# Another order of weighing, adding and score chain, and longer rings, in the edge passes of the first two layers of a graph network

## The reference

```python
# first layer, for each of 2 heads (D = 128), grouped by source node
score = s_src[src] + s_dst[dst]
e = jnp.exp(-jnp.where(score > 0, score, ALPHA * score))
row_sum = segment_sum(e, src);  num = segment_sum(e[:, None] * h[dst], src)
out = elu(num / row_sum[:, None])
...
# second layer, 8 heads of 32, grouped by destination node
alpha = edge_weight[:, None] * (alpha_l[src] + alpha_r[dst])
alpha = jnp.where(alpha > 0, alpha, 0.2 * alpha)
ex = jnp.exp(alpha - segment_max(alpha, dst)[dst])
agg = segment_sum(x[src] * (ex / (segment_sum(ex, dst)[dst] + 1e-16))[:, :, None], dst)
```

## Time and profile before

| | |
|---|---|
| median of 3 runs | 6146.24 us (6140.39 to 6148.77) |
| the profiled execution's own time | 6137.13 us |
| its span | 6135.2 us |
| first layer's edge pass: first gather, last gather, last add | 842.09, 1444.44, 1470.59 us |
| second layer's edge pass: the same | 2214.1, 2820.01, 2864.52 us |
| busy: PE, DVE, ACT, POOL | 3529.9, 3292.3, 1408.6, 3409.4 us |

### The profile page before, as it was taken

How to read it: one execution, slowest core, us unless ns; L and a number is a source line. 1 busy time by engine, 2 the same in 40 slices (tenths; PEclk the granted TensorE clock), 3 DMA queues, 4 the chain that set the end, 5 groups by cost and what they waited for, 6 DMA issues and landing times. The chain is left out here.

```text
span 6135.2 us, 56916 instructions
## 1 busy us (share of the span) xinstructions
PE 3529.9 (58%) x14811; PEld 2769.4 (45%) x14811; DVE 3292.3 (54%) x6546; ACT 1408.6 (23%) x3123; POOL 3409.4 (56%) x3358
## 2 busy tenths in 40 slices
PE   0365237774300067774677775887777667955551
PEld 0265126663100056663455553775555466434441
DVE  7497325555300047767678887347888742122225
ACT  0000112221200022221355553334555332200000
POOL 3778777776788747773066663005666400057771
PEclk9755656775655558876889997998999888977776
DMA  1043134443200034543277775016777610333333
GB/s 42 2 107 75 28 78 130 127 128 51 51 2 2 3 89 132 133 129 68 97 215 201 201 200 135 18 55 198 201 202 200 151 35 22 143 114 100 99 99 49
DMA packets 289802, 630.60 MB, mean 103 GB/s; under 512 B 79692, under 2 KB 134320, under 8 KB 286384
## 3 DMA queue, kind: packets, MB, share of 16 engines
q0 software_dynamic: 168256, 437.11, 29.2%
q1 hardware_dynamic: 121328, 190.89, 9.7%
HBM read 560.35 MB, written 66.48 MB: 102 GB/s over the span
## 5 line engine op out<-in xcount | busy, mean ns | idle before, releaser
L875 PE MATMUL edge_sums<-edge_rows,edge_hot 128*128 128x272 f32 (+3 forms) x4640 | 1575.3, 505 | 767.1 <-issue 285.4
L875 PEld LDWEIGHTS edge_sums<-edge_rows,edge_hot 128*128 128x128 f32 x4640 | 1155.0, 257 | 1087.6 <-issue 369.8
L809 POOL DMA_INDIRECT edge_rows<-kv_rows,dst_index x928 | 877.6, 946 | 1157.7 <-POOLq L89 661.2
L809 POOL DMA_INDIRECT edge_rows<-rel_rows,dst_other_index x464 | 471.0, 1015 | 693.3 <-ACTq L89 552.3
L809 POOL DMA_INDIRECT edge_rows<-xl_rows,dst_index x464 | 465.9, 1004 | 213.6 <-issue 135.2
L809 POOL DMA_INDIRECT edge_rows<-rows,src_index x464 | 462.2, 996 | 156.7 <-issue 131.9
L1141 PE MATMUL edge_own_rows<-dst_x,edge_hot_t 128*128 x1856 | 458.8, 392 | 37.5 <-ACT edge_hot_t L840 21.1
L211 POOL DMA_INDIRECT table_dst<-proj_dst_put_stage x350 | 417.2, 1192 | 98.0 <-issue 86.3
L1141 PEld LDWEIGHTS edge_own_rows<-dst_x,edge_hot_t 128*128 128x128 f32 x1856 | 352.3, 195 | 106.3 <-issue 53.2
L1032 DVE TENSOR_TENSOR edge_rows<-edge_rows,edge_turn_p 128x2048 f32<-128x2048 f32 x174 | 396.6, 2279 | 1.7 <-ACT edge_rows L1250 1.3
L1528 PE MATMUL proj_prod<-proj_w,proj_turned 128*128 128x512 f32 (+1 forms) x900 | 367.2, 554 | 1.0 <-ACT proj_turned L1476 0.9
(11 more groups left out here) (391 smaller groups left out, 5790.3 us busy)
## 6 DMA issues: line engine op xcount, KB each, us to landing
edge_where<-local_dst SPq DMA_DIRECT2D x174, 256.0 KB, 3.4
dst_rank_keys<-in_dst SPq DMA_DIRECT2D x85, 312.5 KB, 3.5
rel_rows<-proj_out SPq DMA_DIRECT2D x25, 1024.0 KB, 3.8
edge_where<-local_src SPq DMA_DIRECT2D x58, 256.0 KB, 3.5
edge_rows<-kv_rows,dst_index POOLq DMA_INDIRECT x928, 3.8
kv_rows<-proj_out SPq DMA_DIRECT2D x50, 260.0 KB, 2.0
edge_rows<-rows,src_index POOLq DMA_INDIRECT x464, 2.9
edge_rows<-xl_rows,dst_index POOLq DMA_INDIRECT x464, 2.9
```

What stands on the lines that cost most here:

```text
L809: pool.indirect_dma_start(out=self.rows[:, h * U + b, 0:self.width], out_offset=None, in_=self.source[:, :], in_offset=bass.IndirectOffset ...
L875: last = nc.tensor.matmul(sums[p % len(sums)][:, 0:width], self.hot[s % 2][:, 2 * (p % 4) + i, :], self.half(s)[:, 2 * (p % 4) + i, first: ...
```

## The change

In the first layer (`source_pass`) the ring grows from 6 batches to 10. DVE's order becomes: bend 0 and mark 0 ahead of the loop; then for each half s weigh s, add the sums of s-1, bend s+1, mark s+1. PE's and ACT's orders stay.

In the second layer (`flash_pass` with `dot` false) the ring grows from 10 batches to 14. The weighing of a chunk and its adds come a step later than before: step f totals chunk f, runs the chain of chunk c = f-1, weighs chunk d = f-2, and adds the second half of chunk g = f-3. One step more is run. The coefficients and the rescaling factor get a PSUM bank of their own (`back_p`), so `turn_scores` waits only for `lowered`; the waits for `copied`, `weighed` and `fixed` move to `scale`. In return `sums` has 4 banks, not 5. PE expands one batch further ahead.

With `dot` true only `scale` differs: it has these three waits too, which `turn_scores` had and keeps.

Semaphores are cleared at 110, not at 120; with the longer rings' 8 more semaphores there are 4 clearings, not 3.

```diff
@@ Phase.__exit__
-        if len(Phase.used) > 120:
+        if len(Phase.used) > 110:
@@ flash_pass
+        ring = RING if dot else 14
-        sums = [ph.ps(f"sums{n}", [P, 512]) for n in range(3 if dot else 5)]
+        sums = [ph.ps(f"sums{n}", [P, 512]) for n in range(3 if dot else 4)]
+        back_p = turn_p[:, P:3 * P] if dot else ph.ps("back_p", [P, 512])
+        factor = link_p[:, 64:72] if dot else back_p[:, P:P + 8]
@@ flash_pass, DVE, step_sum
-                c, d = f - 1, f - 2
+                c, d, g = f - 1, f - 2, f - 3
                 if chunk(c):
                     runs(c)
-                if chunk(d):
-                    tiles = e.node_tiles(nc, dve, 2 * d + 1)
-                    add(8 * d + 4, tiles[0])
-                    add(8 * d + 5, tiles[1])
+                if chunk(d):
+                    weigh(2 * d)
+                if chunk(f):
+                    total(2 * f)
                 if chunk(c):
                     links(c)
                     face(c)
+                if chunk(g):
+                    tiles = e.node_tiles(nc, dve, 2 * g + 1)
+                    for n in range(4):
+                        add(8 * g + 4 + n, tiles[n])
                 if chunk(d):
-                    add(8 * d + 6, tiles[2])
-                    add(8 * d + 7, tiles[3])
+                    tiles = e.node_tiles(nc, dve, 2 * d)
+                    fix(d, tiles[0])
+                    e.mark(nc, dve, 2 * d + 1, summed)
                 if chunk(c):
                     form(c)
                     lower(c)
-                if chunk(f):
-                    total(2 * f)
-                if chunk(c):
-                    e.mark(nc, dve, 2 * c, summed)
-                    weigh(2 * c)
-                    e.mark(nc, dve, 2 * c + 1, summed)
+                if chunk(d):
+                    weigh(2 * d + 1)
+                    dve.wait_ge(fixed, d + 1)
+                    for n in range(3):
+                        add(8 * d + n, tiles[n])
                 if chunk(f):
                     total(2 * f + 1)
                     bend(f)
+                if chunk(d):
+                    add(8 * d + 3, tiles[3])
                 if chunk(c):
-                    weigh(2 * c + 1)
-                    tiles = e.node_tiles(nc, dve, 2 * c)
-                    fix(c, tiles[0])
-                    dve.wait_ge(fixed, c + 1)
-                    for n in range(4):
-                        add(8 * c + n, tiles[n])
+                    e.mark(nc, dve, 2 * c, summed)
@@ flash_pass, PE
             def turn_scores(c):
                 pe.wait_ge(scored, 2 * c + 2)
-                after(pe, copied, copies * 2 * c)
-                after(pe, weighed, 2 * c)
-                after(pe, fixed, c)
+                if dot:
+                    after(pe, copied, copies * 2 * c)
+                    after(pe, weighed, 2 * c)
+                    after(pe, fixed, c)
+                else:
+                    after(pe, lowered, c)
...
             def scale(c):
                 pe.wait_ge(shaped, c + 1)
                 pe.wait_ge(lowered, c + 1)
-                nc.tensor.matmul(link_p[:, 64:72], ...
+                after(pe, copied, copies * 2 * c)
+                after(pe, weighed, 2 * c)
+                after(pe, fixed, c)
+                nc.tensor.matmul(factor, ...
@@ flash_pass, PE, step_sum: the new order
+   turn_scores(c); pairs(2g+1, (0, 1)); send(c); pairs(2g+1, (2, 3))
+   expand(4f+2); expand(4f+3); spread(c); pairs(2d, (0, 1, 2))
+   expand(4f+4); expand(4f+5); pairs(2d, (3,)); scale(c); turn_back(c)
@@ source_pass
-        e = Stream(ph, k, order, order.index, source, W + 2, 6)
+        e = Stream(ph, k, order, order.index, source, W + 2, 10)
@@ source_pass, DVE
+            bend(0)
+            e.mark(nc, dve, 0, summed)
             for s in range(HALVES):
-                bend(s)
+                weigh(s)
                 if s:
                     add(s - 1)
-                e.mark(nc, dve, s, summed)
-                weigh(s)
+                if s + 1 < HALVES:
+                    bend(s + 1)
+                    e.mark(nc, dve, s + 1, summed)
```

More of the change, by code:

```diff
@@ L944, in multiply @@
             def multiply(j):
-                dve.wait_ge(e.arrived[j % RING], 16 * U * (j // RING + 1))
+                dve.wait_ge(e.arrived[j % ring], 16 * U * (j // ring + 1))
                 dve.wait_ge(expanded, j + 1)
-                keys = e.rows[:, j % RING * U:(j % RING + 1) * U, 0:C]
+                keys = e.rows[:, j % ring * U:(j % ring + 1) * U, 0:C]
                 nc.vector.tensor_tensor(keys, own_rows[j % 2][:, :, :], keys, ALU.mult).then_inc(multiplied, 1)
@@ L1107, in step_sum @@
                     bend(f)
+                if chunk(d):
+                    add(8 * d + 3, tiles[3])
                 if chunk(c):
-                    weigh(2 * c + 1)
-                    tiles = e.node_tiles(nc, dve, 2 * c)
-                    fix(c, tiles[0])
-                    dve.wait_ge(fixed, c + 1)
-                    for n in range(4):
-                        add(8 * c + n, tiles[n])
-            for f in range(CHUNKS + 2):
+                    e.mark(nc, dve, 2 * c, summed)
+            for f in range(CHUNKS + (2 if dot else 3)):
                 if dot:
@@ L1209, in step_sum @@
             def step_sum(f):
-                c, d = f - 1, f - 2
+                c, d, g = f - 1, f - 2, f - 3
                 if chunk(c):
                     turn_scores(c)
-                if chunk(f):
-                    expand(4 * f + 1)
+                if chunk(g):
+                    pairs(2 * g + 1, (0, 1))
                 if chunk(c):
                     send(c)
-                if chunk(d):
-                    pairs(2 * d + 1, (0, 1))
+                if chunk(g):
+                    pairs(2 * g + 1, (2, 3))
+                if chunk(f):
+                    expand(4 * f + 2)
+                    expand(4 * f + 3)
                 if chunk(c):
@@ L1221, in step_sum @@
                 if chunk(d):
-                    pairs(2 * d + 1, (2, 3))
+                    pairs(2 * d, (0, 1, 2))
                 if chunk(f):
-                    expand(4 * f + 2)
+                    expand(4 * f + 4)
+                    expand(4 * f + 5)
+                if chunk(d):
+                    pairs(2 * d, (3,))
                 if chunk(c):
@@ L1227, in step_sum @@
                     turn_back(c)
-                if chunk(f):
-                    expand(4 * f + 3)
-                    expand(4 * f + 4)
-                if chunk(c):
-                    pairs(2 * c, (0, 1, 2, 3))
             expand(0)
-            for f in range(CHUNKS + 2):
+            if not dot:
+                expand(1)
+            for f in range(CHUNKS + (2 if dot else 3)):
                 if dot:
```

16 lines of the change are left out of this document (8 added, 8 removed).

## The result

Both kernels ran 20 times on one chip, in turns: before 6139.36 us in the median (6126.67 to 6148.77), after **6146.37 us** (6142.77 to 6155.3). The ratio is 1.0013, with a 95% interval of 1.0007 to 1.0019: slower by 7 or 8 us, less than the 0.2% that I called a change. The profiled execution of after took 6148.08 us, its span is 6146.3 and its mean granted clock 0.76.

What follows compares the result with a forecast made beforehand. POOL's gather issuing was taken to bound both passes. The terms 4 - 2.5 + 0 + 2 + 1.3 = +4.8 us, added to the median of 6146.2, gave 6151 us, range 6134 to 6170, forecast as no change.

Steps and rivals of the forecast that it cites:

- POOL's issuing paces both passes, and the waits for PE are covered: First two layers: POOL's gather issuing sets the pace; DVE's waits for PE run beside it, so removing them gains nothing.
- The first layer's mark, 0.50 us a hold: First layer: at its new place each mark holds a gather 0.50 us instead of 0.42, +4 us over 55 marks.
- That marks hold gathers: Both passes: a gather issued t us into a DVE mark is held for 1.08 - t us.
- The first layer's end, -2.5 us: End of first pass: four adds no longer stand between last total and its mark, so the last add comes 2.5 us earlier.
- The second layer's marks, 0, and end, +2 us: Second layer: moved marks keep the old mean hold of 0.49 us, 0; the pipeline one step deeper costs +2 us at the end.
- One clearing more, +1.3 us: One more clearing of semaphores, with its barrier, costs +1.3 us, between 0.7 and 2.
- The rings, 0: Rings of 10 and 14 in the first two layers: POOL did not wait for places, so 0 us.
- The third layer's three more waits, 0: Third layer: three more waits on PE in each chunk's scale, all met long before: 0, at most +9 us.
- the bad phase: Rival: marks lock where they hold gathers longer in both passes, 6167 us, up to 6184; chance 0.22.
- The gap: Rival: marks start just behind a gather's start and hold nothing, 6097 us in both passes, about 6125 in one; chance 0.09.
- hidden waits for the ring: Rival: the long gathers really wait for ring places, so longer rings remove 23.3 + 27.0 us, 6098 us; chance 0.03.
- A starved POOL: Rival: second layer's sums come 5 us too late for POOL in each of 29 steps, +145 us; chance 0.04.

Runs made afterwards that it cites:

- The filler from PSUM: Changed kernel with a DVE copy of 128x528 out of PSUM between bend and mark in the first layer: 6696.99 us, 0.979 of the kernel before on the same chip.
- the memset ahead of a mark: Changed kernel with a DVE memset between bend and mark in the first layer: 6692.11 us (0.978 of before) with 128x240, 6710.59 us (0.982) with 128x680.
- the short rings: Changed kernel with the rings of before, 6 batches in the first layer and 10 in the second: 7020.33 us, 1.027 of the kernel before.
- the marks on ACT: Changed kernel with ACT writing the marks instead of DVE: 6699.57 us (0.980 of before) in first, second and fourth layer, 6687.94 us (0.978) in first and fourth.

## Why the prediction was right

The time, 6146.37 us, lies in the range of 6134 to 6170, 4.6 under the forecast of 6151, and the forecast of no change over 0.2% held. That it came so near is in part luck: the median that I added the sum to, 6146.2 of 3 runs, is 6.9 us above that of the 20 (6139.36), and the sum was 2 us too small. Step by step:

- **POOL's issuing paces both passes, and the waits for PE are covered: right.** 169 of 173 us of DVE's waits for PE ahead of adds went, no gap of POOL's was over 0.3 us before or after, and first to last gather grew by 1.6 and 2.8 us. I had put DVE's idle ahead of the adds near 0; 40 and 37 us of it stayed, so 155 of the 232 us moved. I named as the condition that DVE's and PE's own loop stays under 10 us a half. The other chips show its far side: there the loop takes longer, since PE's sums are reported late, POOL waits 216 us for sums in the old order of the second pass, and the change gains 2.1%.
- **The first layer's mark, 0.50 us a hold: right in mechanism, 2 us over in the sum.** In 46 of the 58 halves the total started within 3.1 us of the half's last gather, and there the mean hold is 0.50 us, the value that I took. In the other 12 (the start, and halves whose last rows landed late) it is 0.20, which I had left out: POOL's busy time rose 1.7 us, not 4.
- **That marks hold gathers: right.** The Trainium skill ("SBUF — State Buffer", section "Who interferes with whom") has tensor_tensor leave descriptor generation alone, as inferred. The runs decide against it where the descriptors are a gather's: 462.4 us busy with two SBUF inputs, 439.2 with one of them in PSUM. The kernel before had shown it too: in the third layer's two rounds, whose marks ACT makes, its gathers are busy for 439.0 and 438.6 us. The section also says that an instruction with at most one SBUF input, outside the two-port modes, does not contend with GpSimd. The filler from PSUM bears that out (23 of 23 not held); the memset ahead of a mark, which has no input at all, does not (24 of 24 held with 680 columns, 21 of 21 with 240). A memset as such is not enough: the one of 128x6450 that clears `l_acc` at the start of the pass (5.43 us, no mark behind it) leaves the gathers issued in it at 0.94 to 0.97 us. A short one without a mark behind it was never tried.
- **The first layer's end, -2.5 us: right.** Total to last add went from 13.7 to 10.5 us, -3.2. Of it 2.0 us were lost to a later landing of the last rows. Two profiled executions do not tell whether that landing belongs to the kernel.
- **The second layer's marks, 0, and end, +2 us: small, as said.** POOL's busy time rose 2.7 us and the end grew by 1.1, together 3.8 where I had 2.
- **One clearing more, +1.3 us: right,** 1.52 us of wait where 0.33 was.
- **The rings, 0: right here, for a reason that was too short.** I priced the ring of 14 by POOL's beat alone. On the other chips it is half of the only part that pays, and without it the new order costs 2.7%.
- **The third layer's three more waits, 0: open.** From first gather to last add its two rounds take 3.2 and 0.6 us more in the profiled executions (724.9 to 728.2 and 726.5 to 727.0), where I had 0 and at worst 9.
- The sum was +4.8, and the medians show +7 (the interval 4 to 12 us). Single executions of one kernel here differ by 22 us over 20 runs, so terms of 1 to 4 us read from one execution each, the third layer's above all, are not settled.

The rivals: the bad phase needed a mean hold of 0.64 us in the first pass, it is 0.43 over all 58 (463.9 - 438.9 = 25.0 us). The gap did not come, since the marks fell where the working had put them. That the long gathers were hidden waits for the ring fell twice over: longer rings left them as they were, and taking one input to PSUM removed them. (Its price should have read 6097, not 6098: 6151 less the 4 of the first term and the 50.3.) A starved POOL is what the short rings made (1030 us), and what the four batches more prevent.

Three things stay open: why PE's finished work is reported late in the traces of the other chips, and whether the recording has a part in it; what parts PE's single matmuls by 0.7 us there; and what taking away the holds (some 25 us in each of the three passes) would gain on a chip like the first, where POOL paces them. I expected the last from the marks on ACT, and no run met such a chip.

## What to carry to other kernels

A wait that the profile shows is worth something only if the engine that paces the stage has gaps behind it: read the pacing engine's own waits first, in the stage's own window. A decoupling (later sums and a longer ring) bought nothing where sums were reported at once and 2% where they were reported late, so state the condition with the price; its two halves go together, since the later order with the short ring was the worst of all versions. And busy time beyond the count times the undisturbed duration is a finding of its own: here 25 us a pass, removed by moving one operand, which can pay only where that engine is the one that paces (no run here showed the gain). And before "waits for nothing" is read from a trace, compare its number of semaphore events with that of another trace of the same kernel.

## What was not expected of the hardware

- The same kernel takes 6139 us in one set of runs and 6839, 6841 and 6872 on three chips in others, with each set's runs within 0.4% of one another. The first pass of the changed kernel is 66 us longer there. In the traces from there PE's semaphore events come up to 44 us behind the end of the work that they tell of, in bunches 0.06 us apart, and half of all semaphore events are missing.
- A DVE instruction on two SBUF inputs of 128x1024 holds a gather's issue on POOL to its own end plus 0.81 us; with one input in PSUM it holds none. A memset of 128x680 or 128x240 right ahead of it extends the hold to gathers that start in the memset; a copy from PSUM of about the same length does not, nor does a memset of 128x6450 with no mark behind it hold any.
